# Second layer of a two-layer transformer: key blocks added in place, denominators over 256 columns, a causal mask in four quarters, and by-query scores one pair of heads further ahead

## The reference

```python
scale = jnp.asarray(np.sqrt(D_K), x.dtype)            # 16 heads, D_K = 8, D_V = 64
q = (x @ Wq).reshape(B, T, HEADS, D_K).transpose(0, 2, 1, 3)
k = (x @ Wk).reshape(B, T, HEADS, D_K).transpose(0, 2, 1, 3)
v = (x @ Wv).reshape(B, T, HEADS, D_V).transpose(0, 2, 1, 3)
scores = jnp.einsum('bhqd,bhkd->bhqk', q, k) / scale
causal = jnp.triu(jnp.ones((T, T), dtype=bool), k=1)
scores = jnp.where(causal, jnp.asarray(-jnp.inf, scores.dtype), scores)
attn = jax.nn.softmax(scores, axis=-1)
ctx = jnp.einsum('bhqk,bhkd->bhqd', attn, v)
out = ctx.transpose(0, 2, 1, 3).reshape(B, T, HEADS * D_V)
return out @ Wo
```

## Time and profile before

| | before |
|---|---|
| median of 3 runs | 949.31 us (949.01 to 952.53) |
| the profiled execution, its own time | 950.26 us |
| span of its core, first to last instruction | 948.5 us |
| mean granted TensorE clock (1 is 2.4 GHz) | 0.937 |
| TensorE busy in the span | 83% |
| VectorE busy in the span | 61% |
| ScalarE busy in the span | 50% |
| GpSimd busy in the span | 31% |

### The profile page before, as it was taken

How to read it: one execution, slowest core, us unless ns; L and a number is a source line. 1 busy time by engine, 2 the same in 40 slices (tenths; PEclk the granted TensorE clock), 3 DMA queues, 4 the chain that set the end, 5 groups by cost and what they waited for, 6 DMA issues and landing times. The chain is left out here.

```text
span 948.5 us, 19520 instructions
## 1 busy us (share of the span) xinstructions
PE 790.8 (83%) x7061; PEld 451.7 (48%) x7061; DVE 575.1 (61%) x1715; ACT 472.5 (50%) x750; POOL 296.2 (31%) x437
## 2 busy tenths in 40 slices
PE   1588989998829999179999999999999999739970
PEld 0234444444316778125555555555555555534430
DVE  4458999999531111244576776666666656324687
ACT  0377888887812222035454545445455444306664
POOL 3012333333336000424344444434443322100152
PEclk9989999999958999679999999999999999878995
DMA  0274333433215553221454444333334332210002
GB/s 26 72 239 124 97 89 96 108 84 89 69 32 129 158 149 88 67 59 45 96 96 96 96 96 92 74 86 78 81 76 96 79 85 51 56 45 0 1 0 89
DMA packets 111705, 78.02 MB, mean 82 GB/s; under 512 B 12272, under 2 KB 103088, under 8 KB 111616
## 3 DMA queue, kind: packets, MB, share of 16 engines
q1 hardware_dynamic: 107984, 71.16, 30.5%
q0 software_dynamic: 3344, 5.56, 2.2%
q10 hardware_dynamic: 288, 0.13, 0.1%
HBM read 37.86 MB, written 13.63 MB: 54 GB/s over the span
## 5 line engine op out<-in xcount | busy, mean ns | idle before, releaser
L1375 DVE TENSOR_REDUCE l_neg_max<-l_by_query 128x6 bf16<-128x768 f32 x128 | 122.5, 957 | 129.9 <-PE l_by_query L1121 129.6
L1447 POOL TENSOR_SCALAR_AFFINE_SELECT l_probs<-l_probs 128x512 f32<-128x512 f32 x128 | 87.1, 680 | 190.9 <-ACT l_probs L1250 190.7
L493 ACT ACTIVATE l_probs<-l_ps_s,minus_bound 128x1024 f32<-128x1024 f32 x128 | 137.9, 1116 | 2.3 <-PE l_ps_s L367 1.4
L1250 ACT ACTIVATE l_probs<-l_by_key 128x768 f32<-128x768 f32 x128 | 103.8, 811 | 68.1 <-PE l_by_key L1151 63.9
L1166 PE MATMUL l_ps_c<-l_probs,l_values 128*64 128x256 f32 (+1 forms) x1024 | 113.5, 343 | 0.0
L1166 PEld LDWEIGHTS l_ps_c<-l_probs,l_values 128*64 128x64 f32 x1024 | 62.9, 138 | 39.7 <-issue 21.2
L1190 PE MATMUL l_ps_v<-w_o,l_ctx 128*128 128x128 f32 x512 | 68.6, 290 | 15.1 <-DVE l_ctx L1393 15.1
L382 PE MATMUL l_ps_o<-l_probs,l_vpad 128*32 128x256 f32 x1024 | 80.6, 397 | 0.2
L1103 PE MATMUL l_ps_v<-w_v,l_xT 128*128 128x512 f32 x128 | 72.8, 651 | 0.4 <-ACT l_values L1271 0.2
L1190 PEld LDWEIGHTS l_ps_v<-w_o,l_ctx 128*128 128x128 f32 x512 | 62.6, 200 | 20.9 <-DVE l_ctx L1393 15.5
L1271 ACT ACTIVATE l_values<-l_ps_v 128x512 f32<-128x512 f32 x64 | 38.2, 597 | 65.4 <-PE l_ps_v L1103 60.0
(11 more groups left out here) (229 smaller groups left out, 1422.5 us busy)
## 6 DMA issues: line engine op xcount, KB each, us to landing
l_rrep<-rden_d SPq DMA_DIRECT2D x32, 512.0 KB
q_ring<-l_parts SPq DMA_DIRECT2D x192, 64.0 KB
k_ring<-l_parts SPq DMA_DIRECT2D x192, 64.0 KB
w<-in_L_ffn_w_dram SPq DMA_DIRECT2D x32, 256.0 KB, 3.0
disp_d<-zeros SPq DMA_DIRECT2D x8, 320.0 KB, 3.7
l_xin<-in_L_attn_x_dram SPq DMA_DIRECT2D x16, 128.0 KB, 3.1
l_xr<-in_L_attn_x_dram SPq DMA_DIRECT2D x16, 128.0 KB, 2.5
x_d<-l_x SPq DMA_DIRECT2D x16, 128.0 KB, 2.1
```

The lines of the kernel that those rows point to most:

```text
L493: act.activation(probs[c % RING][:, :], ps_s[c % 2][:, :], ACT.Exp, bias=k["minus_bound"][:, :], scale=SCALE).then_inc(probs_sb, 1)
L1250: act.activation(probs[c % P_RING][:, :, 0:N + P], by_key[:, :, 0:N + P], ACT.Exp, scale=SCALE).then_inc(p_sb, 1)
L1375: dve.tensor_reduce(neg_max[:, :, half, :, h].rearrange("p a u -> p u a"), by_query[:, :, 0:3 * P].rearrange("p u (a q) -> p u a q", a=3), ...
L1447: pool.affine_select(out=corners, in_=corners, compare_op=ALU.is_ge, fill=0.0, base=0, pattern=[[0, 4], [1, P]], channel_multiplier=-1).th ...
```

## The change

- **Denominators.** GpSimd has a new call `add_blocks(b, c)`: once `context(b, c)` has read the probabilities, it adds the second key block's 128 columns onto the later half of the first block's 256, in place, for both heads of the pair (128x256 elements). `denominators` then multiplies 256 columns once instead of 256 and 128, and waits for both additions (`both_sb`). `ctx_ps` now counts every pair. The ring `probs` has 6 buffers instead of 4, indexed by (8 b + c) % 6.
- **Mask.** The tile `causal` (128x512) becomes `corner` (128x256), which holds the same 64x64 lower-left pattern for each half of the rows. The two mask matmuls of a `scores_by_query` (K = 128, 128 output rows, 256 columns) become four on quarters of TensorE (K = 64, 64 output rows): 256 columns for output rows 0 to 63, and 128 columns for output rows 64 to 127, where only the later 64 keys of each block are masked. The constants part builds `corner` with two selects behind one more wait.
- **Order.** `scores_by_query` and `maxima` run one pair further ahead: at the end of step b they reach pair 1 of image b + 2 (before: pair 0). `denominators(b, 0..2)` move one step later, and `denominators(b, 3)` moves from the end of step b to the beginning of step b + 1, behind `context(b + 1, 0)`. `x_by_channel(b + 2)` moves behind it. `maxima_by_head(b + 1, 0)` moves one step earlier. On VectorE `reciprocals(b - 1)` comes after `maxima(b + 1, 2)` instead of first; `lower_parts`, `third_input` and `add_expert` change places. ScalarE's and GpSimd's lists follow; GpSimd's `gather(b + 4)` and second `root` come later. SyncE's list is unchanged.

```diff
-P_RING = 4
+P_RING = 6
...
-            pool.affine_select(out=k["causal"][:, :].rearrange("p (a b) -> p a b", b=P),
-                               in_=k["causal"][:, :].rearrange("p (a b) -> p a b", b=P),
-                               compare_op=ALU.is_ge, fill=-1e30,
-                               base=0, pattern=[[0, 4], [-1, P]], channel_multiplier=1).then_inc(cut, 1)
+            pool.wait_ge(cut, 2)
+            for half in range(2):
+                rows = k["corner"][64 * half:64 * half + 64, :].rearrange("p (a b) -> p a b", b=P)
+                pool.affine_select(out=rows, in_=rows, compare_op=ALU.is_ge, fill=-1e30,
+                                   base=0, pattern=[[0, 2], [-1, P]], channel_multiplier=1).then_inc(cut, 1)
...
                     for u in two:
-                        pe.matmul(by_query[:, u, P:3 * P], ident_bf[:, :], k["causal"][:, 0:2 * P],
+                        r = slice(64 * u, 64 * u + 64)
+                        pe.matmul(by_query[0:64, u, P:3 * P], ident_bf[r, r], k["corner"][r, :],
+                                  start=True, stop=False, skip_group_check=True)
+                    for u in two:
+                        r = slice(64 - 64 * u, 128 - 64 * u)
+                        later = by_query[64:128, u, P:3 * P].rearrange("p (a k) -> p a k", k=P)[:, :, 64:P]
+                        pe.matmul(later, ident_bf[r, r], k["corner"][r, :].rearrange("p (a k) -> p a k", k=P)[:, :, 0:64],
                                   start=True, stop=False, skip_group_check=True)
...
-                    if c % 2:
-                        last.then_inc(ctx_ps, 1)
+                    last.then_inc(ctx_ps, 1)
...
                     if j == 0:
                         at_least(pe, rden_sb, b)
-                    for kb, first, q0 in ((0, 0, 0), (1, N, P)):
-                        for g in range(4):
-                            u, e = divmod(g, 2)
-                            last = pe.matmul(ps_d[32 * g:32 * g + 32, q0:N], sums[:, j, :],
-                                             probs[(2 * j + e) % P_RING][:, u, first:first + N - q0],
-                                             start=j == 0 and kb == 0, stop=j == QUADS - 1 and kb == 1)
+                    pe.wait_ge(both_sb, b * PRE + 2 * j + 2)
+                    for g in range(4):
+                        u, e = divmod(g, 2)
+                        last = pe.matmul(ps_d[32 * g:32 * g + 32, 0:N], sums[:, j, :],
+                                         probs[(b * PRE + 2 * j + e) % P_RING][:, u, 0:N],
+                                         start=j == 0, stop=j == QUADS - 1)
                     last.then_inc(sum_ps, 1)
...
             def step(b):
-                x_by_channel(b + 2)
                 scores_by_key(b, 2)
                 context(b, 0)
-                scores_by_query(b + 1, 1)
+                denominators(b - 1, 3)
+                x_by_channel(b + 2)
+                scores_by_query(b + 1, 2)
 
                 scores_by_key(b, 3)
                 context(b, 1)
-                denominators(b, 0)
                 queries_keys(b + 2)
-                scores_by_query(b + 1, 2)
+                scores_by_query(b + 1, 3)
 
                 scores_by_key(b, 4)
                 context(b, 2)
+                denominators(b, 0)
                 values_of(b + 1, 0)
-                scores_by_query(b + 1, 3)
+                scores_by_query(b + 1, 4)
 
                 scores_by_key(b, 5)
                 context(b, 3)
-                denominators(b, 1)
+                maxima_by_head(b + 1, 0)
                 values_of(b + 1, 1)
-                scores_by_query(b + 1, 4)
+                scores_by_query(b + 1, 5)
 
                 scores_by_key(b, 6)
                 context(b, 4)
-                maxima_by_head(b + 1, 0)
+                denominators(b, 1)
                 values_of(b + 1, 2)
-                scores_by_query(b + 1, 5)
+                scores_by_query(b + 1, 6)
 
                 scores_by_key(b, 7)
                 context(b, 5)
-                denominators(b, 2)
                 values_of(b + 1, 3)
-                scores_by_query(b + 1, 6)
+                scores_by_query(b + 1, 7)
 
                 scores_by_key(b + 1, 0)
                 context(b, 6)
+                denominators(b, 2)
                 project(b - 1, 0)
-                scores_by_query(b + 1, 7)
+                scores_by_query(b + 2, 0)
 
                 scores_by_key(b + 1, 1)
                 context(b, 7)
-                denominators(b, 3)
                 project(b - 1, 1)
                 maxima_by_head(b + 1, 1)
-                scores_by_query(b + 2, 0)
+                scores_by_query(b + 2, 1)
...
             def step(b):
+                exponential(b, 2)
                 x_out(b + 2)
-                exponential(b, 2)
 
                 exponential(b, 3)
                 context_out(b, 0)
+
+                exponential(b, 4)
                 high_part(b + 2)
-
-                exponential(b, 4)
                 values_out(b + 1, 0)
 
                 exponential(b, 5)
                 context_out(b, 1)
+                maxima_out(b + 1, 0)
                 values_out(b + 1, 1)
 
                 exponential(b, 6)
-                maxima_out(b + 1, 0)
                 values_out(b + 1, 2)
...
             def step(b):
+                maxima(b + 1, 2)
                 reciprocals(b - 1)
+
                 add_attention(b - 2)
-                maxima(b + 1, 1)
+                maxima(b + 1, 3)
+
+                lower_parts(b + 2)
+                third_input(b - 2)
+                maxima(b + 1, 4)
 
                 add_expert(b + 3)
-                maxima(b + 1, 2)
-
-                third_input(b - 2)
-                lower_parts(b + 2)
-                maxima(b + 1, 3)
+                maxima(b + 1, 5)
 
                 second_input(b + 3)
-                maxima(b + 1, 4)
-
                 divide(b - 1, 0)
                 divide(b - 1, 1)
-                maxima(b + 1, 5)
+                maxima(b + 1, 6)
 
                 divide(b - 1, 2)
                 divide(b - 1, 3)
-                maxima(b + 1, 6)
-
                 maxima(b + 1, 7)
+
                 maxima(b + 2, 0)
+
+                maxima(b + 2, 1)
...
+            def add_blocks(b, c):
+                if real(b):
+                    pool.wait_ge(ctx_ps, b * PRE + c + 1)
+                    pr = probs[(b * PRE + c) % P_RING]
+                    pool.tensor_tensor(pr[:, :, P:N], pr[:, :, P:N], pr[:, :, N:N + P], ALU.add).then_inc(both_sb, 1)
...
             def step(b):
                 mask(b, 2)
+                add_blocks(b, 0)
+                mask(b, 3)
+                add_blocks(b, 1)
                 root(pow3, x3_step, (b - 2) * X3 + 1 + 2 * NB, mv3, veps3, rstd3, b - 2)
-                mask(b, 3)
-                root(pow2, x2_step, (b + 3) * X2 + 3 * NB, mv2, veps2, rstd2, b + 3)
                 mask(b, 4)
+                add_blocks(b, 2)
                 low_part(b + 2)
                 mask(b, 5)
+                add_blocks(b, 3)
+                mask(b, 6)
+                root(pow2, x2_step, (b + 3) * X2 + 3 * NB, mv2, veps2, rstd2, b + 3)
+                add_blocks(b, 4)
+                mask(b, 7)
+                add_blocks(b, 5)
                 gather(b + 4)
-                mask(b, 6)
-                mask(b, 7)
                 mask(b + 1, 0)
+                add_blocks(b, 6)
                 mask(b + 1, 1)
+                add_blocks(b, 7)
```

More of the change, by code:

```diff
@@ L146, in _ @@
             pool.memset(k["tri_bf"][:, :], 1.0).then_inc(filled, 1)
-            pool.memset(k["causal"][:, :], 0.0).then_inc(filled, 1)
+            pool.memset(k["corner"][:, :], 0.0).then_inc(filled, 1)
             pool.iota(iota_base[:, :], pattern=[[CAP, E]], base=0, channel_multiplier=0).then_inc(filled, 1)
@@ L178, in _ @@
             s.did(dve.tensor_copy(k["gate_T"][:, :], gps[:, :]))
-            dve.wait_ge(cut, 3)
+            dve.wait_ge(cut, 4)
             s.did(dve.tensor_copy(k["ident_bf"][:, :], k["ident"][:, :]))
@@ L1024, in l1_layer @@
         key_ps, p_sb, masked, ctx_ps, ctx_sb, sum_ps = (sem(n) for n in ("key_ps", "p_sb", "masked", "ctx_ps", "ctx_sb", "sum_ps"))
+        both_sb = sem("both_sb")
         rden_sb, rden_out, rrep_in, divided, wo_ps = (sem(n) for n in ("rden_sb", "rden_out", "rrep_in", "divided", "wo_ps"))
@@ L1161, in context @@
                     pe.wait_ge(masked, b * PRE + c + 1)
-                    pr = probs[c % P_RING]
+                    pr = probs[(b * PRE + c) % P_RING]
                     for kb, first, q0 in ((0, 0, 0), (1, N, P)):
@@ L1249, in exponential @@
                     at_least(act, sum_ps, b * QUADS + c // 2 - P_RING // 2 + 1)
-                    act.activation(probs[c % P_RING][:, :, 0:N + P], by_key[:, :, 0:N + P], ACT.Exp, scale=SCALE).then_inc(p_sb, 1)
```

(14 more changed lines are left out.)

## The result

The changed kernel takes 995.79 us (median of 6 runs, 994.05 to 1000.71) against 948.35 us: 1.051 times the time before, 95% interval 1.048 to 1.054. It is slower, as forecast (1001; 966 to 1015). The profiled execution took 1000.35 us with a span of 998.6, 50.1 more than the span before.

What follows compares the result with a forecast made beforehand. Two bounds lay together, TensorE (25.3 us) and the image-to-image loop through SyncE's queue (25.5); the change lengthens the loop. Profiled 950.3 + 4 (ends) + 47.5 (13 periods of 29.3 against 25.65) = 1001.8, median 1001, range 966 to 1015.

Steps and rivals of the forecast that it cites:

- The loop: Image-to-image chain of reciprocals, SyncE's queue, maxima rows and key scores: 27.4 us against 25.65, 22.8 us in all.
- R: End of VectorE's reciprocals of the denominators; claimed 14.65 us from there to key(b+1, 0), 5.2 from key(b, 2) to it.
- The clock: TensorE's clock falls to half around the new idle stretch: 2.1 us each, nine images in ten, 1.9 us per image.
- SyncE's queue: Transfers behind rden (rrep, x, twelve loads, maxima rows) move by 2.8 us, order unchanged; R to key(b+1, 0) stays 14.65.
- Denominators: TensorE call without its four matmuls of 128 columns: 0.57 us instead of 0.78, 0.85 us saved per image.
- Additions: Eight new GpSimd additions, 0.65 us each (bounds 0.5 and 1.16), hidden, costing nothing in the sum.
- The ends: Outside the steady images: +4 us before the first image's loop, nothing at the end of the layer.
- The mask: Four quarters on TensorE take 0.22 us, saving 0.11 per call (bounds 0.05 and 0.2), 0.9 us per image.
- The bank rule: Different row tiles can't access one PSUM bank together: would add 0.05 us per mask call, 2 us in all.
- The loop alone: Rival 1: the longer loop without a clock fall, 976 us; chance 0.28.
- Faster: Rival 2: SyncE's queue stops being the bound and TensorE's 23.5 us set the time, 922 us; chance 0.09.
- rival 4: GpSimd additions hold up VectorE's divides, which take the lead: up to 1.2 us per image, 1016 us; chance 0.09.

Runs made afterwards that it cites:

- e1: Changed kernel with reciprocals(b-1) back before maxima(b+1, 2) in VectorE's list; 962.9 us, 1.013 times the kernel before.
- e2: Changed kernel with the first half of the maxima rows sent after the first six of SyncE's twelve loads; 968.3 us, 1.016 times the kernel before.
- e5: Changed kernel with the edits of e1 and e2 together; 948.9 us, 1.000 times the kernel before.
- e10: Kernel before with the mask in quarters and the first half of the maxima rows sent after six loads; 940.8 us, ratio 0.989.
- e11: Kernel before with only SyncE's list reordered, first half of the maxima rows after six loads; 942.4 us, ratio 0.991.
- e6: e5 with all four divides between maxima(b+1, 6) and maxima(b+1, 7) on VectorE; 940.5 us, 0.991 times the kernel before.
- e9: e6 with denominators(b, 3) back at the end of the step, behind project(b-1, 1); 942.9 us, 0.993 times the kernel before.
- e12: e9 with GpSimd's root for the second layer norm before mask(b, 6); 938.6 us, 0.990 times the kernel before.
- e3: Changed kernel with two useless matmuls of 512 columns before each scores_by_query(b+1, 7); 983.0 us, 1.036 times the kernel before.
- e8: Changed kernel with GpSimd only signalling instead of its eight additions per image; 1010.0 us, 1.065 times the kernel before.
- e4: Kernel before with the new order and ring of six, but full mask, old denominators, no additions; 1013.0 us, ratio 1.065.
- e7: Kernel before with only the mask in quarters; 947.6 us, 0.999 times the kernel before.

## Why the prediction was right, and where a size was off

*The loop.* The mechanism held: shortening either of its two segments brought back 33 us (e1) or 28 us (e2), and both together all of it (e5). Predicted 14.65 + 7.55 + 5.2 = 27.4 us without the clock; the five periods without a fall are 27.04 to 28.03, 27.38 in the mean. With the clock I said 29.3 and it is 29.11. The measured terms, in the mean of thirteen: R to key(b+1, 0) 15.16 (said 14.65), key(b+1, 0) to key(b+1, 2) 8.72, of which 7.67 with the clock up (said 7.55), and from there to R 5.23 (said 5.2). The 7.55 had counted on a short wait less, and that was not there.

*The clock.* That it would fall in most images held, but it was 8 of 13 and not nine of ten. One fall cost 1.7 us in the mean (said 2.1), 1.5 to 1.9 and once 2.4. That makes 8.72 - 7.67 = 1.05 us per image where I had 1.9. The prediction oversized this term most, by 0.85.

*SyncE's queue.* The stretch from R to key(b+1, 0) was said not to change. It didn't in the eight images in which rden landed as before, 14.58 in the mean. In five it did by another way: rden took 3.2 to 3.6 us to land, not 1.7, as at 602.15 to 605.58, and there the stretch is 16.08. In the mean of all that is 0.51 us more than said, and nothing in the prediction stood for it. So the 29.11 so near to 29.3 is in part luck: a term that was missing, and two small ones, made up for 0.66 of the 0.85 by which the clock was oversized. The clock fell in all five of these images and in three of the other eight, so part of its share may come of the late landings too; no run separates them.

*Denominators.* 0.57 (597.96 to 598.53), as said. *Additions.* 0.73 us at the median and 0.76 in the mean, said 0.65; hidden but for one wait of 0.68 us at the end of the layer. *The ends.* +3.9 and +1.2, said +4 and 0.

*The mask* is the step that failed: "0.9 us per image". The group's own saving of 0.11 was right to 0.01, but the price of entering the quarters after a full-array call was missing, and what is left is 0.05 (e10 against e11). It did not show in the forecast, since TensorE's own time is not the bound of the changed kernel, and in the loop only two masks count. It did show in later forecasts that rested on TensorE's time: e10 came out 2 us above its range, and e6, 4.5 us above its first range, had counted on 23.5 to 24 us of TensorE. e9 and e12, 8 and 2 us above, were worked out from waits instead; there I had overlooked that the divides stood behind GpSimd's root, and what they take beside its work. The bank rule that the prediction quotes from the Trainium skill would have made the group 0.27; it is 0.22 here (598.90 to 599.12), and both kinds of quarters start at 598.90. That speaks against it, but since the 0.1 for the change of shape was an estimate, the length alone doesn't decide.

*The rivals.* The loop alone (976) lacks the clock's share, 13 x 1.05 = 13.7 us by the stretch; e3 gives some 9 of it back. Faster was ruled out by the chain, as argued. The divides never took the lead in the changed kernel, since each image still waited for the rows. But two divides with an addition beside them did take 1.89 us (0.76 and 1.21), where two without one took 1.28 (616.06), and the addition took 1.15 instead of 0.72. The rule that rival 4 quotes from the Trainium skill has one of the two blocked by the other. The trace agrees in size: the addition from 613.57 got longer by 0.43, with 0.56 of the first divide left, and the second divide by 0.53, with some 0.6 of the addition left when the first had ended:

```profile
613.57 1.15 POOL L1462 TENSOR_TENSOR l_probs<-l_probs 128x256 f32<-128x256 f32 x1
```

```profile
616.06 1.28 DVE L1400 TENSOR_TENSOR l_ctx<-l_ctx,l_rrep 128x512 f32<-128x512 f32 x2
```

Behind the repairs (e5) the divides were in the next wait, behind the root.

## What to carry to other kernels

When two bounds lie on top of each other, work taken from the one gives nothing by itself; look for the cycle from image to image, add up its segments engine by engine, the transfer queue among them, and see which segment each moved call enters. A call that is moved behind another in an in-order list moves everything that hangs on it, here sixteen transfers and the rows behind them. Before making room on TensorE, see where the idle time will gather: here a long stretch cost not only itself but also, in 8 of 13 images, 1.7 us of slower work behind it.

## What the runs showed of the hardware

- Taking work away (e8, 98 us of GpSimd's) made the kernel 14 us slower, and adding useless matmuls (e3) made it 13 us faster (some 9 by the clock), with the granted clock of the steady part at 0.89 and 0.98 against 0.95, and 12 and 3 falls against 8.
- Entering quarters of the array after a full-array call cost 0.1 us, as much as the quarters saved (e10 against e11).
- VectorE divides and a GpSimd addition side by side both got longer: 1.89 us for two divides instead of 1.28, 1.15 for the addition instead of 0.72.
- A 128 KB write to memory took 1.72 us to land in most images, but 3.2 to 3.6 us in five in a row of the changed kernel (541 to 664 us), in some of e2, e3, e4 and e8, and in one of e7 (3.83). In four of the five images with the late landing the twelve loads had no long one among them. What holds it back no run shows; it stays open.
